# Attention output projection computed inside the last attention head: heads 0 to 10 as one product, the last head's share from its own accumulator

## The reference, cut

```
y      = layernorm(x)                                  # eps 1e-6
q,k,v  = split(y @ qkv_w + qkv_b)                      # 12 heads of 32
a      = softmax(q*scale @ k.T + rel_h + rel_w)        # 2304 x 2304 per head
o      = concat_heads(a @ v)                           # 2304 x 384
x      = x + o @ proj_w + proj_b                       # the projection of this change
t      = layernorm(x)                                  # eps 1e-5
gates  = softmax(t @ Wg + bg); keep the best 2 of 8
x      = x + sum_e gate_e * (gelu(t @ W1_e + b1_e) @ W2_e + b2_e)
```

## Time and profile before

| | us |
|---|---|
| median of 3 runs | 2289.35 (2288.3 to 2291.29) |
| the profiled execution | 2290.41 |
| its span, first to last instruction | 2288.7 |
| mean granted PE clock over the span | 0.934 of full |
| PE busy / DVE busy / ACT busy / POOL busy | 2061.9 / 1451.9 / 1502.9 / 923.8 |

### The profile page before, as it was taken

The page is one execution under the profiler, slowest core; times in us unless marked ns, Lnnn a source line. Parts: engine busy times, 40 slices in busy tenths (PEclk is TensorE's granted clock), DMA queues, the critical chain, the costliest instruction groups (busy, mean ns, idle before and its releaser), DMA issues. The chain is left out here.

```text
span 2288.7 us, 34244 instructions
## 1 busy us (share of the span) xinstructions
PE 2061.9 (90%) x11132; PEld 1799.6 (79%) x11132; DVE 1451.9 (63%) x2321; ACT 1502.9 (66%) x2533; POOL 923.8 (40%) x621
## 2 busy tenths in 40 slices
PE   6956479999999999999999999684699999999997
PEld 6932268888888888888888888463688888989997
DVE  5667569999999999999999997376423442120000
ACT  3367058888888888888888889512255555555554
POOL 0051313333333333333333333380555665565553
PEclk9955689999999999999999999787599999999999
DMA  6688835645556455554655454223423533221111
GB/s 211 221 224 251 190 73 96 131 77 115 98 107 124 78 106 112 105 109 75 126 105 104 90 96 99 83 104 115 159 67 108 152 111 112 42 43 29 29 28 15
DMA packets 92822, 247.02 MB, mean 108 GB/s; under 512 B 10168, under 2 KB 44440, under 8 KB 88420
## 3 DMA queue, kind: packets, MB, share of 16 engines
q1 hardware_dynamic: 81024, 223.57, 41.0%
q0 software_dynamic: 10672, 20.46, 5.4%
q10 hardware_dynamic: 960, 0.80, 0.1%
HBM read 179.27 MB, written 65.52 MB: 107 GB/s over the span
## 5 line engine op out<-in xcount | busy, mean ns | idle before, releaser
L895 DVE TENSOR_REDUCE mx<-ps_m 128x1 f32<-128x384 f32 x1212 | 641.9, 552 | 101.5 <-PE ps_m L750 96.2
L607 POOL TENSOR_TENSOR p_lo<-p_f,p_hi 128x768 fp32r<-128x768 f32 x216 | 402.9, 1865 | 714.0 <-ACT p_f L854 714.0
L848 ACT ACTIVATE p_hi<-ps_s 128x768 fp32r<-128x768 f32 x648 | 528.6, 816 | 136.6 <-PE ps_s L764 133.2
L854 ACT ACTIVATE p_f<-ps_s 128x768 f32<-128x768 f32 x648 | 525.8, 811 | 12.8 <-POOL p_lo L607 12.8
L750 PE MATMUL ps_m<-key_hi,query_hi 128*128 128x384 f32 x1240 | 419.5, 345 | 43.9 <-DMA query_hi<-rel_hi_d 31.8
L607 DVE TENSOR_TENSOR p_lo<-p_f,p_hi 128x768 fp32r<-128x768 f32 x432 | 426.9, 988 | 38.6 <-ACT p_f L854 37.6
L761 PE MATMUL ps_s<-query_hi,key_hi 128*128 128x384 f32 x1296 | 338.1, 342 | 11.5 <-DMA query_rest<-m_d 9.5
L774 PE MATMUL ps_o<-p_hi,val 128*65 128x384 f32 x1296 | 331.6, 337 | 5.3 <-POOL p_lo L607 5.2
L764 PE MATMUL ps_s<-query_rest,key_rest 121*128 121x384 f32 x1296 | 331.9, 337 | 0.0
L774 PE MATMUL ps_o<-p_lo,val 128*65 128x384 f32 x1296 | 331.6, 337 | 0.0
L750 PEld LDWEIGHTS ps_m<-key_hi,query_hi 128*128 128x128 f32 x1240 | 232.3, 189 | 89.7 <-DMA query_hi<-rel_hi_d 32.1
(11 more groups left out here) (247 smaller groups left out, 2286.3 us busy)
## 6 DMA issues: line engine op xcount, KB each, us to landing
query_rest<-rel_lo_d SPq DMA_DIRECT2D x36, 864.0 KB
query_rest<-qk_lo_d SPq DMA_DIRECT2D x36, 576.0 KB
query_rest<-qk_hi_d SPq DMA_DIRECT2D x36, 576.0 KB
query_hi<-rel_hi_d SPq DMA_DIRECT2D x12, 864.0 KB, 16.6
w_raw__19867<-w_u SPq DMA_DIRECT2D x12, 768.0 KB, 4.9
w_raw__19868<-w_u SPq DMA_DIRECT2D x12, 768.0 KB, 4.4
w_raw__19869<-w_u SPq DMA_DIRECT2D x12, 768.0 KB, 4.5
w_raw__19870<-w_u SPq DMA_DIRECT2D x12, 768.0 KB, 4.6
```

The costliest lines, as they stand in the source:

```text
L607: engine.tensor_tensor(p_lo[r][:], p_f[idx % 2], p_hi[r][:].bitcast(F32), ALU.subtract).then_inc(lo_done(0, idx)[0], 1)
L848: act.activation(p_hi[r][:], ps_s[:, bank:bank + 2, 0:TB], ACT.Exp).then_inc(hi_ok, 1)
L854: act.activation(p_f[idx % 2], ps_s[:, bank:bank + 2, 0:TB], ACT.Exp).then_inc(f_ok, 1)
L895: dve.tensor_reduce(mx[s // TILES][:, s // 3 % 6, col:col + 1], ps_m[:, c, 0:TB], AX.X, ALU.max).then_inc(mx_ok, 1)
```

## The change

`phase_proj` is gone. Its work stands in `phase_attention`:

- Heads 0 to 10 become one operand of 352 channels plus a row of ones for the bias (`room`, 3 chunks of 128 rows by 2304 tokens). In head 10 SP loads the sums and outputs of heads 0 to 7, DVE takes the reciprocals, SP writes them out and reads them back spread over 32 rows each, and POOL multiplies (`scale`, six times 128 x 768). Heads 8 to 10 follow in the last head (three times 96 x 768).
- In the last head POOL rounds a tile of 128 tokens (`high_part`, 128 x 1152), DVE makes its low part (`low_part`, 128 x 1152), PE multiplies by the weights into `ps_m` (`tail("all", t)`, 9 matmuls), and DVE adds it to `x1` (`added`). 18 tiles stand at units 26 to 48, 4 units for 3 tiles.
- The last head's `ps_o` is split by ACT (`ot_hi`) and DVE (`ot_lo`), multiplied by its 65 rows of weights (`tail("own", t)`, 3 matmuls of 386 columns, one of which is the softmax sum), divided by that sum and added to `x1` by DVE (reciprocal, `scalar_tensor_tensor`), then the statistics. Six tiles stand at units 29 to 34, six at 43 to 48, six behind unit 53.
- POOL splits the projection's weights in head 10; SP loads them between heads 8 and 9.
- The first expert's pieces are loaded and split in `phase_gates`; from the third block on SP's store of a normalised block stands behind a piece whose buffer must have been split.

```
+            def tail(kind, t):
+                n = number_of[kind, t]
+                if n >= 2:
+                    pe.wait_ge(evicted, n - 1)
+                if kind == "all":
+                    pe.wait_ge(low_ok, t + 1)
...
+            def added(kind, t):
+                if kind == "all":
...
+                    dve.wait_ge(tail_mm, n + 1)
+                    dve.tensor_tensor(x1[:, t, :], ps_m[:, n % 2, 0:C], x1[:, t, :], ALU.add).then_inc(evicted, 1)
+                else:
+                    dve.reciprocal(rec[:, t:t + 1], ps_m[:, n % 2, C:C + 1]).then_inc(rec_made, 1)
+                    dve.scalar_tensor_tensor(x1[:, t, :], ps_m[:, n % 2, 0:C], rec[:, t:t + 1], x1[:, t, :], ALU.mult, ALU.add).then_inc(evicted, 1)
+                    if t > 0:
+                        measured(t - 1)
...
+SPLITS_AT = [8, 11, 14, 17]
+SCALES_AT = [32, 35, 38, 41, 44, 47]
+LATE_SCALES_AT = [20, 23, 26]
...
+            steps.setdefault(FIRST_TILE + 4 * t // 3, []).append(("all", t))
+            steps.setdefault((29 + t if t < TPQ else 37 + t) if t < 2 * TPQ else UNITS, []).append(("own", t))
...
+                    if last:
+                        for job in order:
+                            if unit_of[job] == k + 2 and job[0] == "all":
+                                low_part(job[1])
+                        for job in order:
+                            if unit_of[job] == k - 1:
+                                added(*job)
...
             for blk in range(BLOCKS):
+                if 2 <= blk and RAWS + blk - 2 < PIECES:
+                    sp.wait_ge(moe.w_ok, blk - 1)
+                    moe.load_piece(sp, RAWS + blk - 2)
                 sp.wait_ge(xn_ok, blk + 1)
...
+            for i in range(PIECES):
+                moe.split_piece(pool, i)
```

More of the change, by code:

```diff
@@ L540, in sem @@
             return ctx.enter_context(nc.semaphore(name))
-        query_hi = [sb(f"query_hi{i}", [P, S], F32R) for i in range(2)]
-        key_hi = [key_hi0, sb("key_hi1", [P, S], F32R)]
-        key_rest = [key_rest0, sb("key_rest1", [TOP, S], F32R)]
+        query_hi = [sb("query_hi0", [P, S], F32R), far[2]]
+        key_hi = [key_hi0, far[0]]
+        key_rest = [key_rest0, far[1]]
         query_rest = [sb(f"query_rest{i}", [TOP, VARIANTS, QB], F32R) for i in range(QBLOCKS)]
@@ L669, in rest @@
                     sp.wait_ge(s_ok, UNITS * h + TILES * (b + 1))
+                    if h == HEADS - 2 and b == 0:
+                        joins(QBLOCKS * EARLY)
+                        sp.dma_start(flat_early[:], flat(sums_d, 0, EARLY)).then_inc(sums_in, 16)
+                        for c in range(2):
+                            sp.dma_start(room[:, c, :], o_d[c * P:(c + 1) * P, :]).then_inc(early_in, 16)
                     load_rest(h + 1, b)
                     store(h, par, b)
+                    if h == HEADS - 2 and b == 0:
+                        sp.wait_ge(rec_ok, 1)
+                        sp.dma_start(flat(rec_d, 0, EARLY), flat_early[:]).then_inc(rec_out, 16)
+                        sp.wait_ge(rec_out, 16)
+                        sp.wait_ge(w_split, 4)
+                        spread(0, 2, HPT)
+                        spread(1, 3, HPT)
                     if b < 2:
@@ L676, in rest @@
                     load_hi(h + 2, par)
+                else:
+                    sp.wait_ge(s_ok, UNITS * (h + 1))
+                    for g in range(QBLOCKS):
+                        rows = slice(g * TPQ, (g + 1) * TPQ)
+                        sp.dma_start(x1[:, rows, :], x.rearrange("(t p) c -> p t c", p=P)[:, rows, :]).then_inc(x_in[g], 16)
+                    joins(QBLOCKS * (HEADS - 1))
+                    sp.dma_start(flat_late[:], flat(sums_d, EARLY, LATE)).then_inc(sums_in, 16)
+                    sp.wait_ge(scaled, 6)
+                    sp.dma_start(room[0:P - HD, 2, :], o_d[2 * P:C - HD, :]).then_inc(late_in, 16)
+                    sp.wait_ge(rec_ok, 2)
+                    sp.dma_start(flat(rec_d, EARLY, LATE), flat_late[:]).then_inc(rec_out, 16)
+                    sp.wait_ge(rec_out, 32)
+                    spread(2, 3, LATE)
                 load_max(h + 1, 2)
+                if h == HEADS - 4:
+                    load_weights()
             load_hi(0, 0)
@@ L692, in _ @@
             rest(HEADS - 2, 0)
[L694 to L705, removed]
         @block.gpsimd
@@ L732, in head @@
                     n = QBLOCKS * h + idx // TILES - 1
-                    if idx % TILES == JOIN and idx < UNITS and n >= 0:
+                    if idx % TILES == JOIN and idx < UNITS and 0 <= n < QBLOCKS * (HEADS - 1):
                         joined(n)
+                    if h == HEADS - 2:
+                        if idx in SPLITS_AT:
+                            split_weights(SPLITS_AT.index(idx))
+                        if idx in SCALES_AT:
+                            scale(SCALES_AT.index(idx))
+                        if idx == SCALES_AT[-1] + POOL_EVERY:
+                            edge()
+                    if last:
+                        if idx in LATE_SCALES_AT:
+                            scale(6 + LATE_SCALES_AT.index(idx))
+                        for t in range(TILES):
+                            if idx <= unit_of["all", t] - 2 < idx + POOL_EVERY:
+                                high_part(t)
             for idx in range(POOL_EVERY - 1, FIRST - 1, POOL_EVERY):
```

371 lines of the change are left out of this document (196 added, 175 removed).

## The result

The changed kernel takes 2306.66 us, median of 5 runs (2305.79 to 2312.95), against 2290.28 (2288.3 to 2293.31) for the kernel before: ratio 1.0078, interval 1.0061 to 1.0095. It is **slower**, by some 16 us; the forecast was 2282, with a range to 2296. The profiled execution took 2305.79 us, its span is 2304.1, its mean granted clock 0.933 (before 0.934). That mean hides a difference inside the attention. In the kernel before, PE's granted clock stays at 1.00 from head 0 to head 11 (340 to 1460 us).

The account below looks back on a forecast made before the run. PE bounds the last head; the projection stage is a chain of waits. 69.7 us freed, less 35.1, 0.5, 5.2, 2.2, 4.5, 13 and 1.5, leaves 7.7 us less: 2282 us, own range 2275 to 2285, with rivals 2267 to 2296.

Parts of the forecast that it names:

- What bounds the kernel, and what is freed: Between attention and gates: the 80.1 us stretch shrinks to 10.4, freeing 69.7 us; PE is the bound inside the attention.
- PE's new work and the last head: Last head: 198 added matmuls cost 35.1 us, and PE's waits for DVE and POOL 13 us (3 to 35).
- The sign that I named: Low parts running at 1.4 us in the profile after would show the forecast wrong, with the time then 2264.
- One term of the sum: Last head, units 23 to 29: 22.9 us of POOL and DVE work against PE's 18.1, a loss of 4.8 us.
- The third rival: Last head: DVE and POOL take strict turns, costing up to 35 us instead of 13; at 28, 2297 us; chance 0.18.
- The stores: POOL's store waits reach PE: 5.2 us in head 10 (0 to 9), 2.2 in head 9 (0 to 3).
- Head 10, DVE against POOL, and the clock that I left out: Head 10: POOL's scalings make DVE's `p_lo` late, and weight splits add about 0.8: 4.5 us (0 to 11).
- The gates: Six POOL splits fit into its idle time; stores wait for a split and a piece: 1.5 us (0 to 6).
- Heads 0 to 8: Stretch up to unit 14 of head 9: no difference between the kernels, 0 us.
- The chances: Forecast 0.40, waits hidden 0.17, waits eating the gain 0.25, strict turns 0.18; faster 0.57, same 0.25, slower 0.18.

Follow-up runs that it names:

- aligned: The changed kernel with the attention's tiles moved by 32 bytes to begin at multiples of 64 bytes again: 2300.95 us, later 2301.32 us.
- the changed kernel's second execution: The changed kernel run once more, unedited, beside the kernel before: 2311.14 us, ratio 1.0087.
- Three placements of the splits: Changed kernel, gates' splits on DVE: 2310.69 us; on POOL after the last normalisation: 2315.15; tiles at multiples of 64, POOL behind routing, DVE adding biases from PSUM: 2287.68.
- the three experiments that also left the loads' targets off: Changed kernel with only probability and output tiles at multiples of 64: 2311.31 us; with DVE making the gates' splits: 2310.69; with POOL's splits after the normalisations: 2315.15.

## Why the prediction was wrong

- **What bounds the kernel, and what is freed:** right. The stretch behind the last product is 10.6 us, predicted 10.4, own tiles about 1.25 each as predicted, freed 69.5.
- **PE's new work and the last head:** 45.3 us, predicted 48.6. The mechanism was right, its sizes were not: I costed low parts and casts at 128 x 1152 when they are 128 x 384. A low part takes 0.96 in the mean under contention where I reckoned with 1.36 alone and 2 and more beside POOL. The sign that I named, low parts at 1.4 us and then 2264, fails for the same reason. One term of the sum is also wrong by its own prices: PE's 18.1 us for units 23 to 29 repeat the figure of units 29 to 34; 7 x 1.42 + 30 x 0.1775 is 15.3, the term 7.6 instead of 4.8, and the forecast 2284 to 2285. The third rival, strict turns in the last head, did not occur: PE waited 9.4 us there, not 28. But its price rested on the same sizes, so this is no test of strict turns at the true size.
- **The stores:** 5.2 and 2.0 us, predicted 5.2 and 2.2. Right in mechanism and size, and the earlier trace rows did give PE's patience. That the term can be had back by reordering SP's list, which one might read out of it, is wrong: the late reciprocals take it.
- **Head 10, DVE against POOL, and the clock that I left out:** 17.6 us from unit 14 of head 9 to that of head 11; less the stores' 7.2 it is 10.4, predicted 4.5, range up to 11. The contention itself was about rightly sized: PE's waits for DVE's maxima are 6.1 us in these two heads and 1.9 in the kernel before, 4.2 more. What I put at nothing, without a reason, is that PE's clock falls around its long waits: an estimated 3.8 us up to unit 14 of head 11, 5.3 up to the end of head 11. Not every such wait does it: aligned, a wait of 2.8 us in head 9 left the clock at 1.00, and in the changed kernel's second execution one of 3.3 did. The other 2.4 us I cannot place. The row of the kernel before, from 1200 to 1422 us (after, 5.5 of the 6.1 are in the row shown for head 10):

```profile
PE ps_m L750 <- DVE mx L895: 1.9, 8, 0.4
```

  In DVE's timeline after, the first and the last of these three `p_lo` begin beside a `scale` of POOL (from 1367.50 and 1386.90) and the middle one beside none; each one hit takes two to three times its 0.94:

```profile
1368.20 1.97 DVE L653 TENSOR_TENSOR p_lo<-p_f,p_hi 128x768 fp32r<-128x768 f32 x1
...
1371.49 0.94 DVE L653 TENSOR_TENSOR p_lo<-p_f,p_hi 128x768 fp32r<-128x768 f32 x1
...
1387.02 2.80 DVE L653 TENSOR_TENSOR p_lo<-p_f,p_hi 128x768 fp32r<-128x768 f32 x1
```

- **The gates: the step that failed most.** I had 1.5 us (0 to 6) and it was 12.9. I argued that the splits fit into time in which POOL "sat idle" and asked only whether they end ahead of POOL's own work. Whom they hold up meanwhile I did not ask, because I had limited contention to DVE instructions with two SBUF operands. The normalisations have one and went from 512 to 1574 ns. Three placements of the splits show the cause: away from the normalisations these are at 510 to 512 again, and whatever stands beside the splits instead becomes slow, unless it reads PSUM. The Trainium skill, "SBUF — State Buffer", section "Who interferes with whom", says in a later point than the one that I drew on that copy, cast and tensor_scalar can enter faster modes that use the pair of SBUF ports shared by DVE and POOL, and then contend as well. The trace agrees as far as it goes, with 1574 ns beside POOL's split against 512 without; in which mode the instruction ran it does not show. Counted by the rows, DVE lost 18 x 1.06 = 19 us there, and 12.9 reached the choice of the best two.
- **Heads 0 to 8: costed at nothing, and it was 9.4 us** (6.7 in its second execution; between 7.4 and 14.9 in the three experiments that also left the loads' targets off, the 14.9 with three falls of the clock in these heads). The order of the instructions was the same, and I took that for the whole of it. The change moves most tiles of the attention by 32 bytes, and SP's queue then needs some 3% more time for a byte: that makes 5.9 to 6.5 us in heads 0 to 8 in the two executions, and the rest lies ahead of head 0. Nothing in the trace of before could have priced that; it could have been named as an unknown.
- **The chances:** slower had 0.18, all of it on a rival in the last head, which did not occur. Most of the miss came from places that the change only touches in passing, the placement of tiles and a stage into which work was pushed. Without them the kernel would stand near the 2282 that I forecast: the sum of the other rows is -6.9, where I had -9.2. That is in part luck: up to head 11 the clock and the unplaced 2.4 us add what I had not reckoned with, and the oversized last head takes 3.3 of it back.

## What to carry to other kernels

Time in which an engine sits idle is free only for work that shares nothing with those that run then: before POOL is given SBUF work, list what DVE does in that stretch, and put it beside work that reads PSUM, not beside chains of short instructions. When a queue's order is changed to remove a wait, follow each transfer that is pushed back to its first reader; here the whole gain was lost to the next wait. When PE gets new waits, count more than their length: the clock can fall behind them, and the next matmuls then take 0.326 us instead of 0.1775. And when a change moves tiles, compare their addresses before and after.

## What the hardware showed that I had not expected

- When the targets of the loads lie 32 bytes off a multiple of 64, SP's queue takes some 3% more time for a byte: 53.5% of the DMA engines for 75.07 MB against 52.5% for 76.14 MB in the same stretch. The store queued in it lands after 13.7 to 14.1 us instead of 13.3 to 13.6, in the medians of all executions. From head 0 to head 9 this costs 4 to 6 us in the kernel before and in the changed one alike.
- PE's granted clock fell to 0.50 around waits of 3.1, 5.2 and 2.1 us, in the midst of an attention that runs at 1.00, for 3.4 or 6.8 us each time: matmuls then started 0.326 us apart instead of 0.1775.
- A `tensor_scalar` with a single SBUF tile as input is held up by POOL like a subtraction of two, 1574 against 512 ns, while an addition from PSUM and one SBUF tile is not: 0.56 us.
- The delay beside POOL's splits is the same for long and short DVE instructions, so chains of short ones pay most for their length: fifteen comparisons lost 1.1 us each, 19.0 instead of 2.3 us in all, and eighteen normalisations 1.06 each.
